# Reciprocal roots placed and computed differently, and the routing of tokens rebuilt, in a two-layer network kernel

## The reference

```
xn     = (x - mean) / sqrt(var + 1e-5)
scores = xn @ router                      # 8 experts; the best one per token
gate   = sigmoid(best score); each token's gate * xn goes to its expert
out    = shared(xn) + expert(gate * xn)
# second layer: two inner layers with local attention
q = q / norm(q) * q_scale;  k = k / norm(k) * k_scale   # 8 heads of 64
# and inside each inner layer a layernorm before the gated linear unit
```

## Time and profile before

| | |
|---|---|
| median of 3 runs | 2072.57 us (2064.77 to 2075.15) |
| profiled execution | 2064.33 us, its span 2062.5 us |
| granted TensorE clock, mean | 0.933 |
| busy | PE 85%, DVE 62%, ACT 58%, POOL 42% |

### The profile page before, as it was taken

How to read it: one execution, slowest core, us unless ns; L and a number is a source line. 1 busy time by engine, 2 the same in 40 slices (tenths; PEclk the granted TensorE clock), 3 DMA queues, 4 the chain that set the end, 5 groups by cost and what they waited for, 6 DMA issues and landing times.

```text
span 2062.5 us, 38065 instructions
## 1 busy us (share of the span) xinstructions
PE 1760.4 (85%) x12532; PEld 1140.4 (55%) x12532; DVE 1278.5 (62%) x4211; ACT 1186.3 (58%) x3527; POOL 863.4 (42%) x993
## 2 busy tenths in 40 slices
PE   6679988998989888998899888988899797785776
PEld 4358764654566545664566456654566455463454
DVE  4434456566575667566766666666856666857764
ACT  2434547566666666656666675666666565453633
POOL 2633215643445233542544343433453355534640
PEclk9889999999999999999999999999999998897968
DMA  8146510000000000000000000000000000000000
GB/s 235 50 143 224 187 31 1 11 1 1 6 2 17 1 6 1 1 17 1 6 2 17 1 6 2 17 1 5 2 1 11 1 7 1 1 7 0 1 1 11
DMA packets 49724, 53.48 MB, mean 26 GB/s; under 512 B 6386, under 2 KB 42236, under 8 KB 49532
## 3 DMA queue, kind: packets, MB, share of 16 engines
q0 software_dynamic: 7808, 27.79, 4.1%
q1 hardware_dynamic: 41724, 23.26, 3.9%
HBM read 41.60 MB, written 9.44 MB: 25 GB/s over the span
## 4 chain that ended last, share of the span: by engine, by line
PE 47%; DVE 20%; ACT 7%; issue 6%; POOL 1%; DVEq 0%; ACTq 0%; POOLq 0%
PE ps L596 5%; PE ps L658 5%; PE ps L733 3%; PE ps L616 3%; PE ps L575 3%; PE ps L555 3%; DVE p L1042 3%; DVE big L1232 3%; PE ps L640 2%; PE ps L565 2%; DVE ss L1228 2%; PE ps L784 2%; PE ps L630 2%; PE ps L775 2%; PE ps L777 2%
## 5 line engine op out<-in xcount | busy, mean ns | idle before, releaser
L1342 POOL COPY rdx<-rden 128x256 f32<-128x256 f32 x256 | 100.2, 420 | 656.1 <-DVE rden L1059 651.9
L1042 DVE CUSTOM_DVE_ANT_0 p<-ps,mask 128x128 f32<-128x128 f32 (+1 forms) x512 | 152.3, 354 | 209.6 <-PE ps L588 201.8
L1042 DVE CUSTOM_DVE_ANT_0 p<-ps,mask,nrq 128x128 f32<-128x128 f32 x512 | 148.8, 347 | 181.8 <-PE ps L584 181.7
L596 PE MATMUL ps<-ident,p 128*128 128x128 f32 x1280 | 220.9, 297 | 29.2 <-ACT p L873 26.6
L873 ACT ACTIVATE p<-p,nmax 128x128 f32<-128x128 f32 (+1 forms) x512 | 226.3, 442 | 0.0
L872 ACT ACTIVATE p<-p,nmax 128x128 f32<-128x128 f32 x512 | 200.1, 391 | 37.9 <-DVE nmax L1042 37.2
L887 ACT ACTIVATE pt<-ps 128x384 f32<-128x384 f32 (+1 forms) x256 | 111.9, 437 | 190.6 <-PE ps L596 188.6
L733 PE MATMUL ps<-wqkv,hT 128*128 128x512 f32 x384 | 195.2, 617 | 28.5 <-ACT big L952 28.0
L596 PEld LDWEIGHTS ps<-ident,p 128*128 128x128 f32 x1280 | 143.5, 147 | 107.5 <-issue 90.9
L575 PE MATMUL ps<-k,q 64*128 64x128 f32 x1024 | 133.2, 338 | 37.8 <-DVE nmax L1042 17.2
L575 PEld LDWEIGHTS ps<-k,q 64*128 64x128 f32 x1024 | 82.5, 196 | 141.7 <-issue 83.6
(11 more groups left out here) (255 smaller groups left out, 4112.8 us busy)
## 6 DMA issues: line engine op xcount, KB each, us to landing
slots_in<-xn SPq DMA_DIRECT2D x1, 2560.0 KB, 14.3
v<-slots_in SPq DMA_DIRECT2D x20, 128.0 KB, 4.7
slots_out<-v SPq DMA_DIRECT2D x20, 128.0 KB, 1.8
big<-in_x SPq DMA_DIRECT2D x4, 512.0 KB, 6.0
x<-in_x SPq DMA_DIRECT2D x8, 256.0 KB, 3.7
out_x<-x SPq DMA_DIRECT2D x8, 256.0 KB, 2.3
wqkv<-in_wqkv SPq DMA_DIRECT2D x2, 768.0 KB
xn<-in_x SPq DMA_DIRECT2D x6, 256.0 KB, 3.3
```

The costliest lines, as they stand in the source:

```text
L596: last = nc.tensor.transpose(bank[:, j * P:(j + 1) * P], c.p[:, u % 4, j * P:(j + 1) * P], c.ident[:, :])
L1042: last = V.tensor_tensor_reduce(out=c.p[:, u % 4, a:b], in0=bank[:, a:b], in1=mask, scale=scale, scalar=3e38, op0=ALU.add, op1=ALU.min, ac ...
```

## The change

Statistics, root and whitening of x go by two halves of 16 tiles. The identity and the router are loaded behind the first quarter of x, and the weights of queries, keys and values ahead of the constants. The places come from three products with triangular tables, on TensorE ahead of tick 0, in place of the running sums; they are finished before tick 0, and only the slots' experts remain in `route`. ScalarE multiplies the gates (`gated`). The root has 9 operations in place of 11. `rr` writes negative roots and the factor 8 lies in tables, so that `nrq` goes; the segment `rr` of layer 0 moves one tick later for blocks 1 to 6. `tables` moves to tick 9, the waits for late weights from tick 4 to 8. The masks of local attention and the rotary table are scaled by constants to match.

```
-        self.put(at + TILES, "rr", b, l)
+        self.put(at + TILES + (l == 0 and 0 < b < LAST), "rr", b, l)
...
         self.put(0, "route")
-        self.put(3, "tables")
+        self.put(9, "tables")
         for j in range(BLOCKS):
             self.put(j, "scatter", j)
+            if j >= 2:
+                self.put(j - 2, "gated", j)
...
-def newton_rsqrt(nc, link, r, v, scratch):
-
-    link(nc.vector.tensor_scalar(scratch.bitcast(INT32), v.bitcast(INT32), 1, None, ALU.logical_shift_right))
-    link(nc.vector.tensor_scalar(r.bitcast(INT32), scratch.bitcast(INT32), -1.0, RSQRT_MAGIC, ALU.mult, ALU.add))
-    for _ in range(3):
-        link(nc.vector.scalar_tensor_tensor(out=scratch, in0=r, scalar=-0.5, in1=r, op0=ALU.mult, op1=ALU.mult))
-        link(nc.vector.tensor_tensor(scratch, scratch, v, ALU.mult))
-        link(nc.vector.scalar_tensor_tensor(out=r, in0=scratch, scalar=1.5, in1=r, op0=ALU.add, op1=ALU.mult))
+def newton_rsqrt(nc, link, r, v, scratch, t, sign=1):
+
+    a, b, c3 = (sign * x for x in RSQRT_LAST)
+    link(nc.vector.tensor_scalar(r.bitcast(INT32), v.bitcast(INT32), -0.5, RSQRT_MAGIC, ALU.mult, ALU.add))
+    link(nc.vector.tensor_tensor(scratch, r, r, ALU.mult))
+    link(nc.vector.tensor_tensor(scratch, scratch, v, ALU.mult))
+    link(nc.vector.scalar_tensor_tensor(out=r, in0=scratch, scalar=RSQRT_FIRST, in1=r, op0=ALU.add, op1=ALU.mult))
+    link(nc.vector.tensor_tensor(scratch, r, r, ALU.mult))
+    link(nc.vector.tensor_tensor(scratch, scratch, v, ALU.mult))
+    link(nc.vector.tensor_scalar(t, scratch, c3, b, ALU.mult, ALU.add))
+    link(nc.vector.tensor_tensor(t, t, scratch, ALU.mult))
+    return nc.vector.scalar_tensor_tensor(out=r, in0=t, scalar=a, in1=r, op0=ALU.add, op1=ALU.mult)
...
-    def route():
+    def totals():
+        pe.wait_ge(c.const_loaded, c.CONST_LOADS)
         pe.wait_ge(c.hot_ready, 1)
+        bank = c.o_ps[o.slot("tot")]
+        for i in range(2):
+            last = MM(bank[:, i * P:(i + 1) * P], flat(c.hot)[:, i * P:(i + 1) * P], c.tri[:, 2, :], start=True, stop=True)
+        last.then_inc(c.tot_full, 1)
+
+    def places():
+        pe.wait_ge(c.o_done, o.done("tot"))
         bank = c.o_ps[o.slot("cum")]
-        hot = flat(c.hot)
-        MM(bank[:, 0:256], c.tri[:, 1, :], hot, start=True, stop=True)
-        MM(bank[:, 256:512], c.tri[:, 2, :], hot, start=True, stop=True).then_inc(c.cum_full, 1)
+        n = 2 * P
+        for i in range(2):
+            MM(bank[:, 0:n + EXPERTS], c.tot[:, i * P:(i + 1) * P], c.base[:, i, :], start=i == 0, stop=False)
+        MM(bank[:, 0:n], c.tri[:, 1, :], flat(c.hot), start=False, stop=True).then_inc(c.cum_full, 1)
...
-    pe.wait_ge(c.const_loaded, c.CONST_LOADS)
+    pe.wait_ge(c.ident_loaded, 16 * 2)
...
     for t in range(TILES):
+        if t == 3:
+            totals()
         values_of_tokens(0, 0, t)
+    places()
     produce(0, plan.step(0))
...
         if plan.step(tick - 1):
             transposes(plan.step(tick - 1))
-        if tick == 4:
+        if tick == 8:
...
+    def gated(j):
+        act.wait_ge(c.gate_ready, 1)
+        act.wait_ge(c.mm_full, mm.full("rT", j))
+        act.wait_ge(c.xr_ready, j + 1)
+        act.wait_ge(c.xr_pool_ready, j + 1)
+        for t in range(TILES * j, TILES * (j + 1)):
+            last = A(c.xr[:, t, :], c.xr[:, t, :], ACT.Copy, scale=c.gate[:, t:t + 1])
+        last.then_inc(c.gated_ready, 1)
...
+        if t == 2:
+            act.wait_ge(c.best_ready, 1)
+            A(c.gate[:, :], c.best[:, :], ACT.Tanh, scale=0.5).then_inc(c.best_sig, 1)
...
-    act.wait_ge(c.best_ready, 1)
-    A(c.best[:, :], c.best[:, :], ACT.Tanh, scale=0.5).then_inc(c.best_sig, 1)
+    gated(0)
+    gated(1)
...
-        if tick == 4:
+        if tick == 8:
...
-    def route():
-        dve.wait_ge(c.best_sig, 1)
-        TS(c.gate[:, :], c.best[:, :], 0.5, 0.5, ALU.mult, ALU.add).then_inc(c.gate_ready, 1)
...
+    def places():
+        bank = c.o_ps[o.slot("cum")]
+        n = 2 * P
+        link(TS(c.few[:, 64:64 + ALL], c.iota[:, 0:ALL], float(P), None, ALU.mult))
         dve.wait_ge(c.cum_full, 1)
-        bank = c.o_ps[o.slot("cum")]
-        of_tiles = lambda a: a.rearrange("p (t e) -> p t e", e=EXPERTS)
-        link(V.tensor_copy(c.pa[:, :, :], of_tiles(bank[:, 256:512])))
-        link(V.tensor_copy(c.scores[:, :, :], of_tiles(bank[:, 256:512])))
-        a, b = c.pa, c.pb
-        for d in (1, 2, 4, 8, 16):
-            link(V.tensor_copy(b[:, 0:d, :], a[:, 0:d, :]))
-            link(TT(b[:, d:ALL, :], a[:, d:ALL, :], a[:, 0:ALL - d, :], ALU.add))
-            a, b = b, a
-        counts = a[:, ALL - 1, :]
...
-            link(V.tensor_copy(few(to)[:, 0:d], few(at)[:, 0:d]))
-            link(TT(few(to)[:, d:EXPERTS], few(at)[:, d:EXPERTS], few(at)[:, 0:EXPERTS - d], ALU.add))
-            at, to = to, at
-        link(TT(c.cmp[:, :, :], few(at).unsqueeze(1).to_broadcast([P, SLOTS, EXPERTS]),
+        link(TR(few(1), c.cmp8[:, :, :], axis=AX.X, op=ALU.add))
+        eights = c.cmp8[:, :, 0:EXPERTS]
...
         eid = c.few[:, 128:128 + SLOTS]
         link(TR(eid, c.cmp[:, :, :], axis=AX.X, op=ALU.add))
         link(TS(eid, eid, float(EXPERTS - 1), float(P), ALU.min, ALU.mult))
         link(TT(eid, eid, c.col[:, 0:1].to_broadcast([P, SLOTS]), ALU.add))
-        link(V.tensor_copy(c.wix[:, :], eid))
-        link(TT(few(0), few(at), few(0), ALU.subtract))
-        link(TS(few(0), few(0), float(P), -1.0, ALU.mult, ALU.add))
-        link(TT(a[:, :, :], a[:, :, :], c.scores[:, :, :], ALU.subtract))
-        link(TT(a[:, :, :], a[:, :, :], few(0).unsqueeze(1).to_broadcast([P, ALL, EXPERTS]), ALU.add))
-        ins = TT(a[:, :, :], a[:, :, :], of_tiles(bank[:, 0:256]), ALU.add)
-        ins.then_inc(c.o_done, 1)
-        dve.wait_ge(c.o_done, o.done("cum"))
-        link(TT(a[:, :, :], a[:, :, :], c.hot[:, :, :], ALU.mult))
-        pos = c.few[:, 192:192 + ALL]
-        link(TR(pos, a[:, :, :], axis=AX.X, op=ALU.add))
-        V.tensor_copy(c.pos_i[:, :], pos).then_inc(c.pos_ready, 1)
+        V.tensor_copy(c.wix[:, :], eid).then_inc(c.pos_ready, 1)
...
+        dve.wait_ge(c.wo_loaded, 16 * 2)
...
-        newton_rsqrt(nc, link, c.rr[:, :], c.ss[:, :], c.scratch[:, 0, :])
-        TS(c.nrq[:, g % 2, :, :], c.rr[:, :].rearrange("p (t a h) -> p t a h", t=TILES, a=2)[:, :, 0, :], -8.0, None, ALU.mult)\
+        newton_rsqrt(nc, link, c.rr[:, g % 2, :], c.ss[:, :], c.scratch[:, 0, :], c.scratch[:, 1, :], -1)\
...
+    half = ALL // 2
+    for part in range(2):
+        tiles = slice(part * half, (part + 1) * half)
+        for i in (2 * part, 2 * part + 1):
+            dve.wait_ge(c.xr_loaded[i], 16)
+            for t in range(8 * i, 8 * i + 8):
+                last = V.bn_stats(c.stats_all[:, t, :], c.xr[:, t, :])
+        link(last)
...
+        link(TS(var, c.mv_all[:, tiles, 1], 1e-5, None, ALU.add))
+        link(newton_rsqrt(nc, link, c.rstd_all[:, tiles], var, tmp, more))
+        dve.sem_inc(c.stats_ready, 1)
+        for i in range(4 * part, 4 * part + 4):
+            for t in (4 * i, 4 * i + 1):
...
-    dve.wait_ge(c.wo_loaded, 16 * 2)
...
-    link(TR(top, c.scores[:, :, :], axis=AX.X, op=ALU.max))
-    link(TT(c.hot[:, :, :], c.scores[:, :, :], eight(top), ALU.is_equal))
+    link(TT(c.hot[:, :, :], c.scores[:, :, :], eight(c.best[:, :]), ALU.is_equal))
...
-    dve.wait_ge(c.hot_ready, 1)
+    dve.wait_ge(c.best_sig, 1)
+    TS(c.gate[:, :], c.gate[:, :], 0.5, 0.5, ALU.mult, ALU.add).then_inc(c.gate_ready, 1)
+    dve.wait_ge(c.tot_full, 1)
+    V.tensor_copy(c.tot, c.o_ps[o.slot("tot")][:, 0:256]).then_inc(c.o_done, 1)
+    places()
...
     def scatter(j):
         if j == 0:
             pool.wait_ge(c.pos_ready, 1)
-            pool.wait_ge(c.gate_ready, 1)
             pool.wait_ge(c.zero_filled, 16)
-        pool.wait_ge(c.mm_full, mm.full("rT", j))
-        pool.wait_ge(c.xr_ready, j + 1)
-        pool.wait_ge(c.xr_pool_ready, j + 1)
-        x = c.xr[:, TILES * j:TILES * (j + 1), :]
-        link(G.tensor_tensor(x, x, c.gate[:, TILES * j:TILES * (j + 1)].unsqueeze(2).to_broadcast([P, TILES, P]), ALU.mult))
...
     pool.memset(c.hT[:, SEQ:SEQ + 1], 0.0).then_inc(c.hT_zero, 1)
-    pool.wait_ge(c.stats_ready, 1)
     for i in range(BLOCKS):
...
-    for dst, src in ((c.ident[:, :], w["c_ident"]), (c.router[:, :], w["router"]), (c.tri[:, :, :], w["c_tri"]),
-                     (c.iota[:, :], w["c_iota"]), (c.col[:, :], w["c_col"]), (c.rank[:, :], w["c_rank"]),
+        if i == 0:
+            for dst, src in ((c.ident[:, :], w["c_ident"]), (c.router[:, :], w["router"])):
+                sp.dma_start(dst, src).then_inc(c.ident_loaded, 16)
...
+                     (c.below[:, :, :], w["c_below"]), (c.iota[:, :], w["c_iota"]), (c.col[:, :], w["c_col"]),
                      (c.mask[0][:, :], w["c_mask0"]), (c.mask[1][:, :], w["c_mask1"])):
         sp.dma_start(dst, src).then_inc(c.const_loaded, 16)
```

(53 more changed lines are left out.)

56 lines of the change are left out of this document (34 added, 22 removed).

## The result

The changed kernel takes 2015.4 us (median of 4 runs, 2009.9 to 2018.1) where the kernel before takes 2068.9 in the same set: ratio 0.974, 95% interval 0.970 to 0.977, so 2.6% faster. The forecast was 2019, its range 2002 to 2040. The profiled execution took 2009.89 us, with a span of 2008.1. That is 54.4 less than before; the sum had said 48.6. The total came out near, but two of its terms did not, as the experiments show.

What follows compares the result with a forecast made beforehand. TensorE waits for VectorE, then GpSimd, at the start, and bounds the long rest, with waits for VectorE. 2064.3 - 23.6 - 8 - 5 - 12 = 2015.7 us, plus 3 for the runs' median and spread: 2019, range 2002 to 2040.

Steps and rivals of the forecast that it cites:

- The start: Before the experts' stage: slots reach TensorE at 95.4 us instead of 118.97, a gain of 23.6, bounds 17 and 27.
- Statistics by halves: At the start: root ready at 11.9 us instead of 16.9, so TensorE starts at 13.9; gain 5.0, bounds 3 to 5.5.
- Gates on ScalarE: Among the scatters: GpSimd loses 8 multiplications, 8.6 us; ScalarE takes 32 gate operations, 9 us, at 0.28 each.
- first spread of reciprocals in tick 2: Among the scatters: may be late because ScalarE starts two blocks of gates behind; 1.0 us (0 to 3).
- the scatters keep their pace: Rival for the start: ScalarE's gates or exponentials hold GpSimd, the 8.6 us come back, total 2028; chance 0.10.
- Shorter roots: In the turns: fewer chained operations save 8 us at `rr` (bounds 4 and 11) and 5 at `ln2n` (3 and 7).
- beyond the 0.2 above I count none: In the turns: shorter waits save no slow clock stretches beyond the 0.2 us rounded into the 8 at `rr`.
- the clock gives more: Rival: each wait shrinking below 3.6 us also saves its slow stretch, 1 to 2 us in ten places; 2004, chance 0.10.
- `rr` a tick later: In the turns of blocks 1 to 6: the wait for `s_sb` goes; gain 12 us, bounds 4 and 18.
- L1095 at 1034.0 is 2.5 sooner: In the turns of blocks 2 to 5: L1095 comes at 1034.0, not 1036.52; 2.7 us taken per turn, 10.8 in all.
- only the start gains: Rival: moved roots end later, TensorE waits for keys instead of `s_sb`, shorter operations are partly hidden; 2036 us, chance 0.16.
- slower: Rival: the six moved roots collide with GpSimd, costing 45 us and losing the 12; 2075 us, chance 0.03.

Runs made afterwards that it cites:

- `rr` back: The changed kernel with the segment `rr` of blocks 1 to 6, layer 0, put back to its old tick: 2010.9 us, ratio 0.9724.

## Why the prediction was right, and where it wasn't

**The start (23.6 us).** Statistics by halves: TensorE starts at 14.40 (forecast 13.9) and its scores end at 35.01 (33.16 + 1.85; forecast 34.6); undone, the slots came 4.3 us later and the time rose by 7.4, for a term of 5.0. Places: known at 46.01 (forecast 45.1), 0.9 late, half of it from the scores; this is read from the timeline, and no run undid it alone. Gates on ScalarE: four take 1.26 us where I had 1.12. In three traces the whole is 23.6 to 24.0 us, as summed. In the changed kernel's own three profiles it is 16.5, 12.3 and 15.8. The step that failed is the late "first spread of reciprocals in tick 2", taken at 1.0 us (0 to 3): I let only ScalarE's backlog delay the spread. What measured 7.9 us there was VectorE's remote waits, and they hit the second and third spread. So the rival "the scatters keep their pace" came near in the start, where 7 us of its 8.6 came back, but not through ScalarE's gates, and its total of 2028 didn't come. By my own mark, slots after 101 us, this part was wrong in the profile that counted.

By the Trainium skill ("SBUF — State Buffer", Who interferes with whom) I named up to 0.7 us for VectorE's operations beside the first scatters; it was not in the sum, and I wrote that the trace agrees. No trace here shows that rule, by which copies and scalar operations hold back the writing of descriptors. The first scatter takes 1.21 us in the changed kernel, but also in the kernel before, where `route` had ended; the second, beside `route`'s scalar operation L1178 and cast L1180 (from 48.44 and 48.94 us), takes 0.96 like the rest. The one of 1.69 us in the earlier trace rows ran beside `tables`, which holds neither copies nor scalar operations but products of two tensors, and in the kernel before with the short root the scatters beside `tables` take 0.96 and 1.11. Neither that rule nor anything else in my sum had room for a wait of 8 to 14 us.

**Shorter roots (8 + 5 us).** As waits they were right: 13.8 us less idle time from the short root alone, against a sum of 13 that also counted the multiply for `nrq`. As a price they were about half of it. The step that failed is the one on the clock, "beyond the 0.2 above I count none". The kernel before became 29 us (23 to 36) shorter by this edit alone, and the changed kernel owes it 17 to 23. The rival "the clock gives more" had the direction, with 0.10, and deserved most of the chance for this term. Its rule, that a wait which shrinks below 3.6 us saves its slow stretch, did not hold: with `rr` moved, block 3 has waits of 0.50 and 2.24 us and the slow stretch all the same.

**`rr` a tick later (12 us).** This term was wrong. Its instructions came within 0.5 us of where I had put them, and the idle time fell by 8.4 us, inside the bounds of 4 and 18. The time did not change in the kernel before, nor, as far as four runs can tell, in the changed one. The step that failed is "L1095 at 1034.0 is 2.5 sooner", which I took as TensorE's gain: TensorE had still to stand 2.24 us for it, and ran its next stretch at half clock. The rival "only the start gains" named the right term, but put it down to the keys, whose wait grew only from 39.1 to 41.6, no more than it varies between profiles; the new wait is for L1095, 8.9 us.

**Why the total was near.** In part by luck. Behind the first slots I had summed 25 us, nearly all as waits. The three profiles of the changed kernel give 24.4 to 37.9: idle 14.3 to 21.9, and 10.1 to 16.2 of faster matmuls, where I had 0.2. In the first profile 13 us more there stood against 7 less in the start. The shorter root makes 17 to 23 us of it by the timed runs, the moved `rr` none. What is left is of the order of the 9 us that the kernel with the old root shows too (-9.1 in the table). The missing `nrq` multiply is among them: beside "before, `rr` moved", which has the multiply, the old root in the changed kernel has 3.6 us less wait for keys (38.0 against 41.6) and 0.8 less for `down0`'s evacuation. That is within what the keys' wait varies, and no run took the multiply out alone. The moved roots did no harm beside GpSimd, so the rival "slower" did not come; the slow first operations of `rr` in the last turn are as in the earlier trace rows, unmoved.

**What moves.** TensorE works for 177.40 us of the 181 from 102 to 283 us, where the earlier trace rows has 177.90. The experts' stage took nothing back, and `tables` in tick 9 cost nothing that shows.

## What to carry to other kernels

Split a stage into TensorE's busy and idle time before and after an edit: in one pair of profiles each, a shorter dependence chain gave 13.8 us of waiting and 8.5 us of faster matmuls, while a step moved out of one wait into the next gave 8.4 and took 7.6 back. Take a second profile of the same kernel before you trust such a split, and trust most the waits that come out alike in both. An operation taken off a chain pays at every call whose end is waited for, so look for the shortest chain that is exact enough: four operations off the root, in two steps, were worth some 40 us here. When a step is moved, follow TensorE past the first instruction that comes sooner, until the lead is either kept through the next joint or gone.

## What the runs showed that was not expected

When GpSimd issued 32 scatters of 128 rows at 1.26 us each with nothing but a spread of reciprocals between them, VectorE and ScalarE stood for up to 14.6 us between 54 and 110 us in six of nine traces, while TensorE's products that they needed had been done for several microseconds. In the changed kernel VectorE resumed at 70.27 and ScalarE at 70.16, with matmul L602, which VectorE needed, started at 66.65; in its second trace L602 started at 58.34 and VectorE resumed at 70.36. TensorE stood too, 3.16 us ahead of 61.17 in the first, with no releaser named. In both sets in which they occurred, the kernel with some 1 us of GpSimd work ahead of every four scatters had none longer than 0.8 us, at a cost in pace that used up the gain. Whether it is the supply of instructions, the delivery of semaphores or something else on the chip is open: the queues that load instructions moved 5 packets from 54 to 106 us in the changed kernel and 5 in the one with `rr` back, which has no such waits; this does not decide it, and no experiment here separated them. Whether a pause of less than 1 us would do was not tried.

Runs of one kernel differed by up to 16 us with their mean clock (2002 us at 0.948, 2018 at 0.938, `rr` back), which is more than most single terms of the sum.
